# Queue and unit changes in a two-layer conditioned transformer block: max rows sent ahead of the stack reads, statistics and last jobs at other units

## The reference

```python
a_alpha = (t @ attn_alpha_w.T)[:, None, :]
x = x + a_alpha * _attention(_ada_rmsnorm(x, t, attn_gamma_w, attn_beta_w), W_q, W_k, W_v, W_o)
f_alpha = (t @ ffn_alpha_w.T)[:, None, :]
x = x + f_alpha * _swiglu(_ada_rmsnorm(x, t, ffn_gamma_w, ffn_beta_w), gate_w, hidden_w, out_w, out_b)
# then
mean = jnp.mean(input, axis=-1, keepdims=True)
var = jnp.mean(jnp.square(input - mean), axis=-1, keepdims=True)
out = (input - mean) * jax.lax.rsqrt(var + EPS) * weight + bias
tar_bias = jnp.tanh(convInfo @ lin_w.T + lin_b)[:, None, :]
return (out + tar_bias) * weight + bias
```

## Time and profile before

| | |
|---|---|
| median of 3 runs | 821.73 us (821.41 to 822.71) |
| the profiled execution | 823.76 us, its span 821.8 us |
| mean granted TensorE clock | 0.958 of full speed |
| PE busy | 734.0 us (89% of the span) |
| DVE, ACT, POOL busy | 531.9, 469.8, 401.1 us (65%, 57%, 49%) |
| chain that ended last, by engine | PE 69%, DVE 9%, DMA 7%, issue 5%, ACT 4%, POOL 3% |

### The profile page before, as it was taken

How to read it: one execution, slowest core, us unless ns; L and a number is a source line. 1 busy time by engine, 2 the same in 40 slices (tenths; PEclk the granted TensorE clock), 3 DMA queues, 4 the chain that set the end, 5 groups by cost and what they waited for, 6 DMA issues and landing times.

```text
span 821.8 us, 17472 instructions
## 1 busy us (share of the span) xinstructions
PE 734.0 (89%) x6646; PEld 496.0 (60%) x6646; DVE 531.9 (65%) x789; ACT 469.8 (57%) x854; POOL 401.1 (49%) x501
## 2 busy tenths in 40 slices
PE   4777879789998999899999999899989999998886
PEld 3423233445676667666676667666766667677785
DVE  3566467567766676768667776677767776345555
ACT  3346466567656666567665666566655665742331
POOL 3244232145338563666248462656356544763833
PEclk9769698999999999999999999999999999999998
DMA  6755465437441654335442644236333530221110
GB/s 183 255 195 172 139 201 163 155 90 216 132 148 54 214 138 166 106 105 198 127 156 59 243 144 155 66 132 193 118 130 106 187 99 14 81 82 51 47 47 26
DMA packets 63499, 108.74 MB, mean 132 GB/s; under 512 B 10192, under 2 KB 17800, under 8 KB 63416
## 3 DMA queue, kind: packets, MB, share of 16 engines
q1 hardware_dynamic: 62744, 106.91, 41.2%
q10 hardware_dynamic: 544, 0.52, 0.2%
q0 software_dynamic: 128, 0.20, 0.1%
HBM read 59.60 MB, written 39.09 MB: 120 GB/s over the span
## 4 chain that ended last, share of the span: by engine, by line
PE 69%; DVE 9%; DMA 7%; issue 5%; ACT 4%; POOL 3%; SPq 2%; POOLq 0%; ACTq 0%; DVEq 0%
PE ps_x L1254 15%; PE ps_o L1227 12%; PE ps_j L1144 11%; PE ps_j L1267 9%; PE ps_s L1214 9%; PE ps_m L1199 6%; DVE mx L970 3%; DMA qs<-m_hl 2%; PE ps_o L1267 2%; ACT prob L803 2%; DMA stack_scratch<-qk_lo 2%; DMA n_x<-n 1%; PE ps_m L1254 1%; PE ps_s L1254 1%; DVE fx L952 1%
## 5 line engine op out<-in xcount | busy, mean ns | idle before, releaser
L970 DVE TENSOR_REDUCE mx<-ps_m 128x2 f32<-128x1024 f32 x222 | 271.6, 1223 | 140.6 <-PE ps_m L1199 140.1
L803 ACT ACTIVATE prob<-ps_s 128x1024 f32<-128x1024 f32 x256 | 261.7, 1022 | 98.0 <-PE ps_s L1214 97.3
L1214 PE MATMUL ps_s<-qs,ks 64*128 64x512 f32 x512 | 124.0, 480 | 30.9 <-ACT prob L803 16.1
L1214 PEld LDWEIGHTS ps_s<-qs,ks 64*128 64x128 f32 x512 | 49.7, 190 | 156.3 <-issue 83.4
L1227 PE MATMUL ps_o<-prob,v 128*32 128x512 f32 x1024 | 143.1, 632 | 0.0
L565 POOL TENSOR_TENSOR xr<-xr,sc 128x512 f32<-128x512 f32 x43 | 56.0, 1303 | 110.3 <-DVE sc L982 59.6
L1199 PE MATMUL ps_m<-ks,qs 64*128 64x512 f32 x444 | 94.7, 422 | 10.9 <-DVE mx L970 8.0
L540 POOL TENSOR_TENSOR a_lo<-act_y,a_hi 128x256 fp32r<-128x256 f32 x100 | 73.4, 734 | 54.9 <-ACT a_hi L834 54.7
L1254 PE MATMUL ps_x<-n,gh_hi 64*128 64x256 f32 x872 | 98.7, 286 | 1.6 <-DVE act_y L1017 1.6
L1254 PE MATMUL ps_x<-n_x,gh_hi 64*128 64x256 f32 x872 | 94.8, 277 | 2.2 <-DMA n_x<-n 2.2
L1254 PEld LDWEIGHTS ps_x<-n,gh_hi 64*128 64x128 f32 x872 | 75.7, 188 | 12.1 <-DVE act_y L1017 8.0
(11 more groups left out here) (175 smaller groups left out, 1447.5 us busy)
## 6 DMA issues: line engine op xcount, KB each, us to landing
qs<-stack_scratch SPq DMA_DIRECT2D x32, 512.0 KB, 4.1
ks<-stack_scratch SPq DMA_DIRECT2D x32, 512.0 KB, 5.0
stack_scratch<-qk_hi SPq DMA_DIRECT2D x56, 256.0 KB, 2.9
out_scratch<-o_raw SPq DMA_DIRECT2D x32, 256.0 KB, 2.2
n_x<-n SPq DMA_DIRECT2D x32, 256.0 KB, 3.7
stack_scratch<-qk_lo SPq DMA_DIRECT2D x28, 256.0 KB, 3.2
xa<-in_x SPq DMA_DIRECT2D x8, 512.0 KB, 4.2
on_lo<-out_scratch SPq DMA_DIRECT2D x16, 256.0 KB
```

The lines of the kernel that those rows point to most:

```text
L803: act.activation(prob[:, n % 2, 2 * h:2 * h + 2, :], ps_s[:], ACT.Exp, scale=SCALE).then_inc(p_r, 1)
L970: dve.tensor_reduce(mx[:, group % 2, :, h, qt], max_pair(mp)[:], AX.X, ALU.max).then_inc(mx_red, 1)
L1214: mm = pe.matmul(ps_s[:, s, :], ks[r:r + 64, g, j, kb * P:(kb + 1) * P], qs[r:r + 64, g, j, :], start=True, stop=True)
```

## The change

The order of the work and the engine of some of it is changed; the arithmetic is the same.

- SP: `stack_read(b + 1, 0)` goes from unit 6 to unit 7, and `stack_read(b + 1, 2)` from unit 14 to unit 15, so both stand behind the max rows of their old unit.
- Unit 8: ACT's two `square2` of half 0 go ahead of the copy of `o_raw`, right behind the unit's second exponential. POOL's `norm2` of half 0 comes from unit 9 into unit 8, ahead of the addition of WO 1.
- DVE's `statistics` of half 0 go from unit 9 (ahead of unit 10's maxima) to unit 10, behind its maxima and its gate; those of half 1 from unit 15 to unit 0 of the next batch, likewise. POOL's `moments` and `normalise` follow by one unit.
- `MOVED` gives four last jobs other units: FT 1 of sequence 6 from unit 129 to 125, WO 0 and 1 of sequence 7 from 135 and 136 to 134 and 135, FT 1 of sequence 7 from 145 to 141. The transfers `swap_halves` of half 1 and its low halves follow the job.
- The tail: for sequence 7 DVE adds WO to `xr` itself, right behind `scale`, and for the FT jobs of the tail makes the low halves right behind `yf_copy`. ACT makes `fx` (two activations a half) where POOL did; POOL keeps the roots.

```diff
--- before.py
+++ after.py
@@ -46,11 +46,17 @@
        ("V", 1, 0), ("COEF", 1, 0), ("TAB", 0, 0), ("MT", 0, 0), ("TR", 0, 1)]
 
 
+MOVED = {("FT", 1, B - 2): NU - 3, ("FT", 1, B - 1): NU + 13, ("WO", 0, B - 1): NU + 6, ("WO", 1, B - 1): NU + 7}
+MOVED_TO = {n: job for job, n in MOVED.items()}
+
+
 def job_at(n):
 
+    if n in MOVED_TO:
+        return MOVED_TO[n]
     kind, i, d = SCHEDULE[n % UNITS]
     b = n // UNITS + d
-    return (kind, i, b) if n >= 0 and 0 <= b < B else None
+    return (kind, i, b) if n >= 0 and 0 <= b < B and (kind, i, b) not in MOVED else None
 
 
 JOBS = PRO + [job_at(n) for n in range(LAST) if job_at(n)]
@@ -413,8 +419,8 @@
                     store(b - 3, 1)
                 if at(2, -2):
                     load_tab_b(b - 2)
-                if at(2, -2):
-                    swap_halves(b - 2, 1)
+                if job_at(n - 1) and job_at(n - 1)[:2] == ("FT", 1):
+                    swap_halves(job_at(n - 1)[2], 1)
                 if at(2, 0):
                     max_rows(b, 1)
                 if at(3, -1):
@@ -427,7 +433,7 @@
                     o_write(b, 0)
                 if at(5, 1):
                     stack_write(b + 1, 1)
-                if at(6, 1):
+                if at(7, 1):
                     stack_read(b + 1, 0)
                 if at(6, 0):
                     max_rows(b, 2)
@@ -455,9 +461,9 @@
                 if at(13, 1):
                     stack_write(b + 1, 3)
                 if at(14, 1):
+                    max_rows(b + 1, 0)
+                if at(15, 1):
                     stack_read(b + 1, 2)
-                if at(14, 1):
-                    max_rows(b + 1, 0)
                 if at(15, 3):
                     load_xa(b + 3)
                 if at(15, 0):
@@ -564,11 +570,14 @@
                 xs = xr[:, b % 2, 2 * h:2 * h + 2]
                 pool.tensor_tensor(xs, xs, sc[:], ALU.add).then_inc(x_add, 1)
 
+            def root2(b, h):
+                pool.wait_ge(sq2, 2 * (2 * b + h + 1))
+                root(rstd2[:, h], ss2[:, h], EPS_RMS, rstd2_r)
+
             def norm2(b, h):
 
                 hf = 2 * b + h
-                pool.wait_ge(sq2, 2 * (hf + 1))
-                root(rstd2[:, h], ss2[:, h], EPS_RMS, rstd2_r)
+                root2(b, h)
                 pool.wait_ge(rstd2_r, hf + 1)
                 if hf > 0:
                     pool.wait_ge(n2_lo_r, 2 * hf)
@@ -642,27 +651,22 @@
                 def at(k, d):
                     return u == k and 0 <= b + d < B
 
-                if at(0, -3) and b - 3 < B - 1:
-                    moments(b - 3, 1)
-                    normalise(b - 3, 1)
                 if at(0, 1):
                     n_low(b + 1, 0)
                 if at(1, 1):
                     n_low(b + 1, 1)
-                if at(2, -2):
-                    n2_low(b - 2, 1)
+                if job_at(n - 1) and job_at(n - 1)[:2] == ("FT", 1) and n < NU:
+                    n2_low(job_at(n - 1)[2], 1)
                 if at(4, -1):
                     o_norm(b - 1, 1)
-                if at(9, -1):
-                    norm2(b - 1, 0)
-                if at(10, -1):
+                if at(10, -1) and n < NU:
                     n2_low(b - 1, 0)
-                if at(10, -2):
+                if at(11, -2):
                     moments(b - 2, 0)
                     normalise(b - 2, 0)
                 if at(10, 2):
                     root1(b + 2)
-                if at(12, -1):
+                if at(12, -1) and n < NU:
                     norm2(b - 1, 1)
                 if at(13, 0):
                     o_norm(b, 0)
@@ -673,6 +677,8 @@
                 if n in PIECE_AT:
                     split_piece(PIECE_AT.index(n))
                 if at(1, -3) and b - 3 < B - 1:
+                    moments(b - 3, 1)
+                    normalise(b - 3, 1)
                     weigh(b - 3, 1)
                 if at(1, 0) and b > 0:
                     v_copy(b, 3)
@@ -680,10 +686,15 @@
                     o_low(b - 1, 1)
                 if at(6, -2) and n >= NU:
                     add_to_x(("H", 2 * (b - 2)))
-                if at(7, -1):
+                if at(7, -1) and n < NU:
                     add_to_x(("WO", 0, b - 1))
-                if at(8, -1):
+                if at(8, -1) and n < NU:
+                    norm2(b - 1, 0)
                     add_to_x(("WO", 1, b - 1))
+                if n == NU + 7:
+                    root2(B - 1, 0)
+                if n == NU + 9:
+                    root2(B - 1, 1)
                 if at(9, -1):
                     add_bias(b - 1, 0)
                 if at(11, -2):
@@ -736,6 +747,15 @@
                     if b > 0:
                         act.wait_ge(rstd2_r, 2 * (b - 1) + h + 1)
                 square(xr[:, b % 2, 2 * h + t], ss2[:, h, t:t + 1], sq2)
+
+            def norm2(h):
+
+                hf = 2 * (B - 1) + h
+                act.wait_ge(rstd2_r, hf + 1)
+                act.wait_ge(n2_lo_r, 2 * hf)
+                for t in range(2):
+                    act.activation(fx[:, t, :], xr[:, (B - 1) % 2, 2 * h + t], ACT.Copy, scale=rstd2[:, h, t:t + 1])\
+                       .then_inc(fx_r, 1)
 
             def norm1(b, t):
 
@@ -893,6 +913,9 @@
                     tanh(e)
                 if n < NU:
                     exps(n, 1)
+                if at(8, -1) and n < NU:
+                    square2(b - 1, 0, 0)
+                    square2(b - 1, 0, 1)
                 if job_at(n) and GH_AT <= n < NU:
                     evac(job_at(n), n)
                 if u == 0 and 0 < n <= NU:
@@ -913,13 +936,20 @@
                     square1(b + 2, u - 4)
                 if 11 <= u < 15 and 0 <= b + 2 < B:
                     norm1(b + 2, u - 11)
-                if at(8, -1):
-                    square2(b - 1, 0, 0)
-                    square2(b - 1, 0, 1)
-                if at(9, -1):
+                if at(9, -1) and n < NU:
                     square2(b - 1, 1, 0)
-                if at(10, -1):
+                if at(10, -1) and n < NU:
                     square2(b - 1, 1, 1)
+                if n == NU + 7:
+                    square2(B - 1, 0, 0)
+                    square2(B - 1, 0, 1)
+                if n == NU + 8:
+                    norm2(0)
+                if n == NU + 9:
+                    square2(B - 1, 1, 0)
+                    square2(B - 1, 1, 1)
+                if n == NU + 11:
+                    norm2(1)
 
             for n in range(LAST):
                 unit(n)
@@ -951,6 +981,22 @@
                 for k in range(KC):
                     dve.tensor_scalar(y_f[:, k, :], ps_j[:, k * HT:(k + 1) * HT], coef[:, 2, k, b:b + 1],
                                       coef[:, 3, k, b:b + 1], ALU.mult, ALU.add).then_inc(yf_r, 1)
+
+            def n2_low(h):
+
+                hf = 2 * (B - 1) + h
+                for k in range(KC):
+                    dve.wait_ge(yf_r, 2 * hf + k + 1)
+                    dve.tensor_tensor(n2_lo[:, h, k, :], y_f[:, k, :], n2_hi[:, h, k, :].bitcast(F32), ALU.subtract)\
+                       .then_inc(n2_lo_r, 1)
+
+            def add_to_x(h):
+
+                b = B - 1
+                dve.wait_ge(sc_r, SC_NO["WO", h, b])
+                dve.wait_ge(xr_in[h][b % 2], 16 * (b // 2 + 1))
+                xs = xr[:, b % 2, 2 * h:2 * h + 2]
+                dve.tensor_tensor(xs, xs, sc[:], ALU.add).then_inc(x_add, 1)
 
             def max_low(b, g, bank):
 
@@ -1070,8 +1116,12 @@
                     max_low(b, i, mt_bank(n))
                 elif kind == "WO":
                     scale(job)
+                    if b == B - 1:
+                        add_to_x(i)
                 elif kind == "FT":
                     yf_copy(b, i)
+                    if n >= NU:
+                        n2_low(i)
 
             def unit(n):
                 b, u = n // UNITS, n % UNITS
@@ -1092,6 +1142,10 @@
                     scale(("H", 2 * (b - 2) + 1))
                 if 0 <= e < TAIL:
                     gate(e)
+                if at(10, -2):
+                    statistics(b - 2, 0)
+                if at(0, -3) and b - 3 < B - 1:
+                    statistics(b - 3, 1)
                 if chunk_at(n) is not None:
                     scale(("F", chunk_at(n)))
                 if job_at(n) and n < NU:
@@ -1100,10 +1154,6 @@
                     o_recip(b - 1, 1)
                 if at(11, 0):
                     o_recip(b, 0)
-                if at(9, -2):
-                    statistics(b - 2, 0)
-                if at(15, -2) and b - 2 < B - 1:
-                    statistics(b - 2, 1)
                 if TAIL <= e - 1 < NE:
                     a_low(e - 1)
                 if TAIL <= e < NE:
```

## The result

The changed kernel takes 783.94 us (median of 4 runs, 780.83 to 784.21), the kernel before in the same runs 822.22 us (821.41 to 823.41): a ratio of 0.9518, 95% interval 0.9495 to 0.9541, some 39.6 us less.

A forecast was written before the change was run, and what follows sets the result against it. PE, holding 69% of the chain of waits, was taken as the bound, by its stalls and slow clock. Max rows 10, clock 6, units 8 to 10 16.4, statistics elsewhere 0, tail 9.5: 821.7 - 42 = 780 us, range 772 to 797.

The forecast's parts named there:

- Max rows, 10 us: PE's four stalls after unit 0: 3.2 us saved at each of two, the last two gone whole; between 8.5 and 12.4.
- the moved reads cost nothing: Stack reads go out about 1 us later; the first max_scores using them stands three units later, over 10 us.
- Transfer time: Max rows: at most 2.67 us from issue to PE's use, bounded by the pair at 98.34 us.
- Clock, 6 us and 2.5 in the tail: Half-clock stretches behind PE's stalls: 3.5 us back behind the longest, 2.5 for shorter ones, 2.5 more in the tail.
- second rival: Stalls shrink but the 0.50 clock stretches stay in number and length: 788 us, chance 0.10.
- Units 8 and 9, 14.9 us: Earlier squares remove PE's waits: 2.06 us in each of six batches, 2.5 us in the first.
- Statistics, 0.3 us a batch: Unit 10's wait for maxima goes only in part, 1.5 us in all; in units 15 and 0, zero gain.
- Tail, 9.5 us: Waits for n_x and fx go (2.2, 3.95, 2.1 us), clock gives 2.5, remaining n_x wait and ACT cost 0.7 and 0.5.
- third rival: Tail: six two-input instructions put on DVE are each stretched by 0.88 us beside POOL: 785 us, chance 0.05.
- first rival: DVE and ACT have less slack, so max_scores waits more for maxima: 796 us, chance 0.14.
- signs of being right: Max rows within 1 us of low maxima, waits under 2 us; fx under 2; batch 2.5 shorter; one tail n_x wait.
- signs of being wrong: In order: maxima waits above 15 us; mean clock 0.96; DVE's two-input tail instructions over 1 us; ACT idle before squares.

The follow-up runs named there:

- write-first run: Changed kernel with the write of o_raw issued ahead of the stack read in units 8 and 0: 777.98 us, ratio 0.9454.
- the run that sets them apart: Changed kernel with o_raw's write ahead of the stack read, plus POOL's second last-sequence addition waiting for DVE's last a_lo: 774.71 us, ratio 0.9411.
- the last version: Changed kernel with o_raw's write ahead of the stack read, POOL's last addition behind a_lo, half 1's statistics in unit 2: 771.30 us, ratio 0.9386.

## Why the prediction was right

783.94 us lies 4 us above the forecast of 780 and within the range of 772 to 797. The mechanisms were the ones forecast but for SP's queue behind the moved reads, and that the total is so near is in part luck: 3.3 us too much for the max rows stand against 2.7 too little for the statistics and 1.8 for the clock. Term by term:

- **Max rows, 10 us: the path behind them was wrong, 6.7 us measured.** The four stalls that it aimed at lost 11.4 us, and at unit 8 all went as said. The premise of "nothing is ahead of them but a wait for the maxima" was true of the moved pair only; "the moved reads cost nothing" looked at PE, which uses the stack later, and not at what SP issues next. The write of `o_raw` now follows the second stack read by 1.3 us, and SP's read of the denominators waits for it with the max rows queued behind. Two stalls, 5.0 us, stand at units where before there was none. The write-first run takes the lateness away and, in its own trace, both stalls; in two later traces a transfer of 3.8 and 4.3 us leaves 1.1 and 1.6 us at unit 12.
- **Transfer time.** The prediction took the bound of 2.67 us from issue to use. At unit 8 the trace now has 1.82 us, from the issue's end at 77.25 to PE at 79.07. The Trainium skill's figure of some 2.0 us ("DMA: Bandwidth & Descriptors", fixed cost of a transfer) was nearer to that than the bound; by the pair's second issue, which starts at 76.7, it is 2.4 us. The Trainium skill gives the figure for transfers of POOL's own queue, and these are SP's. At unit 12, beside other traffic, the same pair needs 3.65 us.
- **Clock, 6 us and 2.5 in the tail: right to low.** 10.3 us, worked out above. What the prediction did not weigh is that the stretches at 168, 342 and 523 us stand behind waits for `fx`, so that a part of this term belongs to the squares (their run alone gave 4 to 5 us more than its waits). The second rival, same clock as before, is refuted: the mean of the profiled execution went from 0.958 to 0.976, and no execution of the change is below 0.974.
- **Units 8 and 9, 14.9 us: right.** 2.37 us in unit 9 where the sum had 2.06, in the steady batches; the first batch's wait went from 3.05 to 0.87 us. The 0.31 us more were not traced.
- **Statistics, 0.3 us a batch: the reason given for it failed.** It is 0.83, in five batches 4.2 us where the sum had 1.5. "FT's evacuation stays ahead of the maxima, so only part of the wait goes" was argued and not shown; the move alone gives 6.93 us in unit 10 with that evacuation in place. For half 1, "the statistics push the same wait from unit 0 into unit 1" was right to 0.01 us. That "unit 15 and 0" have no room was the right reason: unit 1 has none either, unit 2 has.
- **Tail, 9.5 us: the sum right, its parts not.** 9.1 us behind unit 127, less 0.35 us in unit 125. The wait between FT 0 and its swapped halves did not grow to 2.1, it shrank to 0.5, as FT, halves and low parts all come sooner. Against that stand new waits, 2.5 us for `a_lo` and 1.2 for `on_lo`.
- **Contention, the third rival: true, elsewhere.** The instructions put on DVE keep their times (0.69 us for the addition, 0.42 for the low half). It is `a_lo` that is long, six times at 1.28 to 1.49 us, always beside a TENSOR_TENSOR of POOL; PE waits for two of them. The price is some 1.1 us for the last one, by the run that sets them apart.
- **Waits under other names, the first rival.** With squares alone there are 2.4 us more of them; the statistics' move takes these away again, which is why the whole change shows 5.5 us and not 10.
- **The signs named beforehand.** FT's waits for `fx` (0.9 us), the batch (2.93 us shorter) and the waits for `n_x` (one) came as said, and no `max_scores` of the batches waited for a moved read. Two signs of being right failed: max rows were issued 1.8 and 1.5 us behind their maxima, and one wait for them is 3.13 us. Of the signs of being wrong the third showed, with `a_lo` at over 1 us, and the fourth once, in the tail, where ACT is idle for 1.57 us ahead of the squares.
- **Sums that don't come out.** With the 4.8 and 3.65 us of the first two stalls as limits, a transfer of 2.0 us makes the term for max rows 11.4 us and not 10.9, and with 3.24 us it is 9.2 and not 8.5. The upper bounds of max rows and clock together give 774.6 and not 772. None of this moves the forecast.

The parts measured alone (9.5, 19, 5.0) and the tail's 9.1 sum to 43 us where 39.6 were measured: they add, within their intervals, though the tail's part is read from a trace and not from a run.

## What to carry to other kernels

Where a stall goes on an engine that issues for others, list what its queue issues in the next ten microseconds: transfers that the stall had kept apart now stand together, and a small write behind a large read can hold the queue until it has landed, if something behind it waits for it. Short work that makes an engine late is not gone when it is put a unit on: measure the unit behind it, and put it where the other engine has a long job. A part of a gain may be clock, so look for half-clock stretches behind each wait that is to go.

## What the runs showed of the hardware

- The write of 256 KB landed in 2.0 us with little other traffic, in 6.6 us when issued 1.3 us behind 1 MB of reads, and in 3.1 us when issued ahead of them.
- The pair of 8 KB transfers was used 1.8 us behind the end of its issue at unit 8, 3.65 at unit 12 of the change, and 3.8 and 4.3 us there in two runs with the write ahead of the reads, though two others with that same order show at most 2.7.
- `a_lo` took 1.49 us beside POOL's addition, 0.42 us without it. It ended 0.28 us behind POOL's instruction, and so did all the six long ones in this tail. The `a_lo` at 747.24 us, begun 0.10 us ahead of POOL's pair at L618, kept its 0.42 us, and there the pair took 1.30 us where it takes 1.09 at 419.36 us. The Trainium skill ("SBUF — State Buffer", who interferes with whom) says that a DVE instruction with two SBUF inputs contends with a POOL instruction that reads SBUF, and that the one which comes second is blocked until the first is done. The trace agrees on who is held, whichever begins second; the 0.28 us are less than the 0.42 that `a_lo` takes alone, so not all of it has to wait.
- The clock did not fall behind every wait. The same 1.51 us for `fx` had half clock behind it in two of six batches. In the last version 3.41 us at 0.50 stand at 138 us with only waits of under 0.9 us in the 20 us before. Why there, no run tells.
